# A two-layer block on one core: a batch's Gelu moved into the next batch, the second attention pass unbroken, key rankings back to back

## The reference

```python
# x: (16, 256, 128)
qkv = layernorm(x) @ w_attn                  # 16 query heads of 8 channels, one shared key and value head
att = softmax(causal(q @ k.T / sqrt(8)))     # 256 x 256 for each head
x = x + (att @ v) @ w_proj
xn = rmsnorm(layernorm(x)) * gamma
sim = (xn @ wq.T) against keys               # 8 heads x 2 lists of 32 scores for each token
sx, sy = top16(sim[0]), top16(sim[1])        # the sixteen best of each list
scores, pk = top16(sx + sy over all pairs)   # the sixteen best pairs
h = gelu(xn . table_down[pairs]) * softmax(scores)
x = x + sum over pairs of h * table_up[pairs]
```

## Time and profile before

| | |
|---|---|
| median of three runs | 1045.94 us |
| profiled execution | 1047.43 us |
| its span (first to last instruction) | 1045.6 us |
| DVE busy | 862.4 us (82%) |
| PE busy | 766.0 us (73%) |
| ACT busy | 712.7 us (68%) |
| POOL busy | 644.5 us (62%) |
| chain that ended last, by engine | DVE 38%, PE 34%, issue 16%, ACT 8% |
| mean granted PE clock | 0.887 |

### The profile page before, as it was taken

How to read it: one execution, slowest core, us unless ns; L and a number is a source line. 1 busy time by engine, 2 the same in 40 slices (tenths; PEclk the granted TensorE clock), 3 DMA queues, 4 the chain that set the end, 5 groups by cost and what they waited for, 6 DMA issues and landing times.

```text
span 1045.6 us, 22349 instructions
## 1 busy us (share of the span) xinstructions
PE 766.0 (73%) x6066; PEld 482.5 (46%) x6066; DVE 862.4 (82%) x4054; ACT 712.7 (68%) x1040; POOL 644.5 (62%) x371
## 2 busy tenths in 40 slices
PE   3772868777877878787778878787878778776374
PEld 2431535454554645454455545444545546353243
DVE  2316298998989899899989899989989897988987
ACT  1352686877778686878867786868787786847371
POOL 2111069494958768594939677694949486675851
PEclk9686888899998989898998989898999989897766
DMA  5322103021211103020212112030212111000000
GB/s 148 50 24 35 17 9 43 1 40 15 39 16 35 20 9 47 0 52 3 40 15 39 16 21 34 8 47 0 43 12 39 16 34 18 1 12 2 5 1 10
DMA packets 51538, 26.51 MB, mean 25 GB/s; under 512 B 5168, under 2 KB 51120, under 8 KB 51312
## 3 DMA queue, kind: packets, MB, share of 16 engines
q1 hardware_dynamic: 51504, 26.11, 15.1%
HBM read 19.93 MB, written 5.24 MB: 24 GB/s over the span
## 4 chain that ended last, share of the span: by engine, by line
DVE 38%; PE 34%; issue 16%; ACT 8%; DMA 1%; SPq 1%; POOL 1%; DVEq 1%; ACTq 0%; POOLq 0%
DVE prob L930 13%; PE misc L1156 7%; PE score L1136 5%; PE score L1217 4%; ACT prob L650 4%; DVE late_scores L792 4%; DVE cand_left L894 4%; PE misc L1158 3%; PE score L1138 3%; DVE best L888 3%; DVE best L902 2%; DVE cand L873 2%; PE misc L1245 2%; DVE halves L786 2%; PE score L1229 2%
## 5 line engine op out<-in xcount | busy, mean ns | idle before, releaser
L451 POOL TENSOR_TENSOR acc<-acc,prob 128x1024 f32<-128x1024 f32 x186 | 440.0, 2366 | 16.6 <-DVE prob L930 0.5
L930 DVE SCALAR_TENSOR_TENSOR prob<-score,cut,prob 128x1024 f32<-128x1024 f32 x256 | 317.8, 1277 | 39.3 <-ACT prob L650 38.7
L650 ACT ACTIVATE prob<-score,neg_lse,unit 128x1024 f32<-128x1024 f32 x256 | 296.9, 1198 | 36.2 <-PE score L1217 25.5
L1217 PE MATMUL score<-sel,pieces_t 128*128 128x512 f16 x512 | 176.3, 442 | 73.4 <-DVE prob L930 64.0
L562 ACT ACTIVATE probs<-score 128x512 f32<-128x512 f32 x192 | 107.4, 599 | 65.4 <-PE score L1138 63.8
L438 POOL TENSOR_TENSOR pieces<-sim,pieces 128x512 f16<-128x512 f32 x32 | 36.4, 1159 | 145.1 <-ACT pieces L606 145.1
L1136 PE MATMUL score<-q_stack,k_stack 128*128 128x512 bf16 x192 | 76.3, 401 | 45.7 <-DVE prob L930 23.3
L1217 PEld LDWEIGHTS score<-sel,pieces_t 128*128 128x128 f16 x512 | 42.0, 109 | 145.6 <-DVE prob L930 111.7
L1106 PE MATMUL score<-k_ahead,q_ahead 128*128 128x256 bf16 (+1 forms) x512 | 75.8, 253 | 31.0 <-ACT late_scores L545 13.6
L424 POOL TENSOR_TENSOR scale<-bounded,half_neg 128x2 f32<-128x2 f32 x16 | 11.2, 699 | 130.6 <-DVE bounded L833 130.6
L850 DVE MATCH_REPLACE8 left<-top,sim 128x32 f32<-128x32 f32 x512 | 82.8, 173 | 0.0
(11 more groups left out here) (122 smaller groups left out, 1618.9 us busy)
## 6 DMA issues: line engine op xcount, KB each, us to landing
q_ahead<-q_scratch SPq DMA_DIRECT2D x96, 64.0 KB
q_stack<-q_scratch SPq DMA_DIRECT2D x96, 64.0 KB
q_scratch<-qk_piece SPq DMA_DIRECT2D x16, 192.0 KB, 2.4
xin<-x SPq DMA_DIRECT2D x16, 128.0 KB, 4.4
xres<-x SPq DMA_DIRECT2D x16, 128.0 KB, 4.8
out<-fin SPq DMA_DIRECT2D x16, 128.0 KB, 5.3
k_ahead<-qk_piece SPq DMA_DIRECT2D x96, 4.0 KB
k_stack<-qk_piece SPq DMA_DIRECT2D x96, 4.0 KB
```

What stands on the lines that cost most here:

```text
L451: eng.tensor_tensor(acc[:, j, :], so_far, prob[:, j * FH + h, :], ALU.add).then_inc(acc_added, 1)
L650: eng.activation(prob[:, g, :], score[g % BUFS][:, :], ACT.Exp, bias=neg_lse[:, j, h:h + 1], scale=unit[:, :]).then_inc(prob_made, 1)
L930: eng.scalar_tensor_tensor(prob[:, g, :], score[g % BUFS][:, :], cut[:, j, h:h + 1], prob[:, g, :], ALU.is_ge, ALU.mult).then_inc(prob_mas ...
L1217: ins = eng.matmul(score[g % BUFS][:, cols], pieces_t[:, j, h, :], sel[:, cols], start=True, stop=True)
```

## The change

Six things are done together.

1. The Gelu of batch i is taken in iteration i+1, after the twelve Exps of the second pass, ahead of `invert_sums`. Its matmuls (`hidden_units`) are spread over the second pass: four chunks of tile 1 before the first step, then one chunk after each of the twelve steps, in place of the `keep_busy` matmuls. They read `xn_kept`, a copy of `xn_t`.
2. The two residual copies (`age_x2`, `copy_x2`) and the new copy `keep_xn` are DMAs on SP's queue; they were activations.
3. `weigh_values` waits no longer for `pieces_back`, and no transposes or copies stand inside the second pass. `pieces_back` of both tiles goes in between the first pass's copies, and both use `misc[0]`.
4. On PE `project_y`, the first `piece_transposes` and the first `acc_transposes` stand after two of the first pass's twelve steps; the other ten come behind them.
5. On DVE the rankings of both tiles stand back to back, then `ln1`, `sum_pairs(0)`, `select_pairs(0)`, and only then `make_y`. The gates come later, and `fold_max` comes after `select_pairs(1)` and the second gate, where it stood before `sum_pairs(1)`.
6. In the mask stretch ACT takes `best_exp(1)` before the first `pair_probs`, `log_sum(1)` after it, and spreads the copies of the key scores; on POOL two additions come ahead of `sim_low_piece`.

```diff
@@ SP @@
+            def age_x2(b):
+                copied = held(eng, every(x2_copied, b))
+                read = held(eng, at(fin_made, b, 0))
...
+                eng.dma_start(x2_aged[:, :, :], x2_kept[:, :, :]).then_inc(x2_moved, 16)
+            def keep_xn(b):
+                made = held(eng, every(xn_t_made, b))
+                used = held(eng, at(hidden, b, 0))
...
+                eng.dma_start(xn_kept[:, :], xn_t[:, :]).then_inc(xn_kept_in, 16)
             def iteration(i, d, f, a, m, p):
+                if d and f:
+                    age_x2(i - 1)
+                if f:
+                    copy_x2(i)
@@ ACT @@
                 if a:
-                    for u in range(10):
+                    for u in range(MAX_STEPS):
                         att_exp(i + 1, u)
-                if f:
-                    pieces_back(i, 0)
-                if a:
-                    for u in range(10, MAX_STEPS):
-                        att_exp(i + 1, u)
-                if f:
-                    pieces_back(i, 1)
                 if d and f:
-                    age_x2(i - 1)
-                if f:
-                    copy_x2(i)
+                    activate(i - 1, 0)
+                    activate(i - 1, 1)
                 if a:
                     invert_sums(i + 1)
                 if m:
                     copy_v(i + 2)
-                    for u in range(9):
+                    max_scores_back(i + 2, 0)
+                    max_scores_back(i + 2, 1)
+                if f:
+                    best_exp(i, 0)
+                if m:
+                    for u in range(2, 5):
                         max_scores_back(i + 2, u)
                 if f:
-                    best_exp(i, 0)
+                    pieces_back(i, 0)
+                if m:
+                    for u in range(5, 9):
+                        max_scores_back(i + 2, u)
+                if f:
+                    log_sum(i, 0)
+                    pieces_back(i, 1)
                 if m:
                     for u in range(9, MAX_STEPS):
                         max_scores_back(i + 2, u)
...
+                if f:
+                    best_exp(i, 1)
                     pair_probs(i, 0, 0)
+                    log_sum(i, 1)
                     pair_probs(i, 0, 1)
                 if a:
                     sim_back(i + 1, 0)
+                if f:
+                    pair_probs(i, 0, 2)
+                if a:
                     sim_back(i + 1, 1)
@@ DVE @@
                 if f:
                     select_keys(i, 0)
-                if d:
-                    gate(i - 1, 0)
-                if f:
                     select_keys(i, 1)
                 if p:
                     ln1(i + 3)
-                if a:
-                    make_y(i + 1)
                 if f:
                     sum_pairs(i, 0)
                     select_pairs(i, 0)
                 if a:
+                    make_y(i + 1)
+                if f:
+                    sum_pairs(i, 1)
+                if a:
                     make_x2(i + 1)
                 if d:
+                    gate(i - 1, 0)
+                if f:
+                    sum_best(i, 0)
+                    select_pairs(i, 1)
+                if d:
                     gate(i - 1, 1)
                 if f:
-                    sum_best(i, 0)
+                    log_sum_exp(i, 0)
                 if m:
                     fold_max(i + 2, 0, 6)
                 if f:
-                    sum_pairs(i, 1)
-                    log_sum_exp(i, 0)
-                    select_pairs(i, 1)
-                if f:
+                    sum_best(i, 1)
                     mask(i, 0, 0)
+                    log_sum_exp(i, 1)
                     mask(i, 0, 1)
@@ PE @@
+                if a and d:
+                    hidden_units(i - 1, 1, range(0, 4), xn_kept)
+                for u in range(MAX_STEPS):
+                    if a:
                         scores_for_probs(i + 1, u)
-                        keep_busy(misc[0], 2)
+                    if d and f:
+                        if u < 4 and a:
+                            hidden_units(i - 1, 1, range(4 + u, 5 + u), xn_kept)
+                        elif u >= 4 and a:
+                            hidden_units(i - 1, 0, range(u - 4, u - 3), xn_kept)
...
+                if a:
+                    weigh_values(i + 1, 0, max_t_made, i + 1)
+                    weigh_values(i + 1, 1, max_t_made, i + 1)
+                if m:
+                    scores_for_max(i + 2, 0)
+                    scores_for_max(i + 2, 1)
+                if a:
+                    if f:
+                        eng.wait_ge(pair_step, at(pair_step, i, SUM_STEPS))
+                    project_y(i + 1, y_t_made, i + 1)
+                if f:
+                    if a:
+                        piece_transposes(i, 0, y_t_made, every(y_t_made, i + 1))
...
                 if d:
                     acc_transposes(i - 1, 0)
...
                 if m:
-                    for u in range(4):
+                    for u in range(2, 7):
                         scores_for_max(i + 2, u)
```

More of the change, by code:

```diff
@@ L711, in iteration @@
                     log_sum(i, 0)
+                    pieces_back(i, 1)
+                if m:
+                    for u in range(9, MAX_STEPS):
+                        max_scores_back(i + 2, u)
+                if a:
+                    xn_back(i + 1)
+                if f and not a:
                     activate(i, 0)
                     activate(i, 1)
-                if a:
-                    xn_back(i + 1)
                 if f:
+                    best_exp(i, 1)
                     pair_probs(i, 0, 0)
+                    log_sum(i, 1)
                     pair_probs(i, 0, 1)
@@ L720, in iteration @@
                     sim_back(i + 1, 0)
-                    sim_back(i + 1, 1)
-                if f:
-                    best_exp(i, 1)
                 if f:
@@ L1204, in pair_scores @@
                     eng.wait_ge(piece_t_made, at(piece_t_made, b, j + 1))
-                if g < 2:
+                if g < 2 and not a:
                     eng.wait_ge(act_made, at(act_made, b, g + 1))
+                elif g < 2:
+                    if later(b):
+                        eng.wait_ge(gated, at(gated, b - 1, g + 1))
                 elif g == 2 and m:
@@ new lines, in iteration @@
+                if d and f and not a:
+                    hidden_units(i - 1, 1, range(CH), xn_kept)
+                    hidden_units(i - 1, 0, range(CH), xn_kept)
+                if a:
+                    weigh_values(i + 1, 0, max_t_made, i + 1)
[3 more added lines that the diff above has]
+                    scores_for_max(i + 2, 1)
+                if a:
+                    if f:
+                        eng.wait_ge(pair_step, at(pair_step, i, SUM_STEPS))
+                    project_y(i + 1, y_t_made, i + 1)
@@ L1322, in iteration @@
+                if m:
+                    for u in range(7, 9):
+                        scores_for_max(i + 2, u)
                 if d:
@@ L1324, in iteration @@
                 if m:
-                    for u in range(8, MAX_STEPS):
+                    for u in range(9, MAX_STEPS):
                         scores_for_max(i + 2, u)
+                if f and not a:
+                    hidden_units(i, 0, range(CH), xn_t)
+                    hidden_units(i, 1, range(CH), xn_t)
                 if f:
-                    hidden_units(i, 0)
-                    hidden_units(i, 1)
+                    pair_scores(i, 0, 0, a, m)
+                    pair_scores(i, 0, 1, a, m)
                 if a:
-                    xn_transpose(i + 1, y_t_made, i + 1)
+                    xn_transpose(i + 1, piece_t_made, i)
                 if f:
-                    for h in range(3):
-                        pair_scores(i, 0, h, a, m)
+                    pair_scores(i, 0, 2, a, m)
                 if a:
```

113 lines of the change are left out of this document (46 added, 67 removed).

## The result

| | before | after |
|---|---|---|
| median | 1045.01 us (1043.91 to 1047.60, 4 runs) | 1094.68 us (1092.76 to 1095.91, 4 runs) |
| ratio | | 1.047, 95% interval 1.0444 to 1.0496 |
| span of the profiled execution | 1045.6 us | 1092.8 us |
| DVE, PE, ACT, POOL busy | 862, 766, 713, 645 us | 862, 762, 704, 635 us |
| mean granted PE clock | 0.887 | 0.85 |

The account below looks back on a forecast made before the run. The time to xhat_back plus 20.2 us was taken to set each batch, with late first-pass copies delaying fold_max. Twelve batches 3.4 us longer (40.4) less 2 for edges took 1045.6 to 1084 us; range 1055 to 1098.

Parts of the forecast that it names:

- The ruler: Loop batch: lasts as long as it takes to reach ACT's copy xhat_back, plus an unchanged 20.2 us.
- `make_y` at 17.3: DVE: make_y starts without a wait 17.3 us after the batch's first ranking, against 17.1 before.
- `ln1` 1.17: DVE ahead of make_y: ln1 counted at 1.17 us, its length in the trace of before.
- POOL's additions hold DVE: Rival before make_y: additions ending after 17 hold DVE's two-SBUF steps, 2 us more a batch, 1108 us; chance 0.08.
- The clock: PE's gap before project_y: half rate adds 0 to 1.8 us ahead of the first pass's third step, taken as 1.6.
- everything stays at full clock: Rival on PE: no throttling, fold_max starts at 28.1, a batch is 59.8, total 1065 us; chance 0.22.
- `fold_max` at 29.7: DVE: fold_max starts 29.7 us into the batch, after waiting for ACT's first-pass copies; DVE itself is there at 26.8.
- the sign of 1 us: DVE at fold_max's first step: a new wait of 1 us or more for ACT's copies would show the forecast right.
- The mask stretch: From fold_max's start to xhat_back: 11.55 us, with log_sum(1) and the copies queued behind sum_best(1); xhat_back at 41.2.
- Edges: Iterations 0 and 13 to 15, outside the loop: -3, 0, -3 and +4, together -2 us, bounds -8 and +4.
- The sum: Whole kernel: twelve batches times 3.4 is 40.4, edges -2, so a span of 1084.0 us from 1045.6.
- The costs put at nothing: Residual activations leaving ACT, three DMAs on SP, Gelu matmuls for dummies, Gelu's place: each forecast at no time.

Follow-up runs that it names:

- e1: Kernel after plus 44 dummy matmuls on PE in the gap before project_y; 1068.39 us, ratio 1.0227 to the kernel before.
- e2: Kernel after with best_exp(1) on ACT ahead of the first pass's last three copies and sum_best(1) on DVE ahead of fold_max; 1053.05 us, ratio 1.0085.
- e3: Kernel after with make_y ahead of sum_pairs(0) on DVE again; 1058.52 us, ratio 1.0125.
- e4: Kernel after with the whole of ln1 moved behind make_y on DVE; 1058.89 us, ratio 1.013.
- e5: Kernel after with only ln1's last instruction, the 128x2 tensor_scalar, moved behind make_y; 1080.08 us, ratio 1.0341.
- c13: Kernel after with both the 44 dummy matmuls on PE and make_y ahead of sum_pairs(0); 1057.81 us, ratio 1.0119.
- b_y_late: Kernel before with one edit, make_y moved behind select_pairs(0); 1055.40 us, ratio 1.0088.
- c_best2: c_best, but best_exp(1) behind the first pass's last three copies and sum_best(1) between fold_max's second and third step; 999.48 us, ratio 0.9562.
- c23: Kernel after with best_exp(1) and sum_best(1) early and make_y ahead of sum_pairs(0); 1025.72 us, ratio 0.9811.
- c_best: Kernel after with e2's edit, make_y between sum_pairs(0) and select_pairs(0), and ln1 behind select_pairs(0); 1016.10 us, ratio 0.9724.

## Why the prediction was right, and what was off

The prediction was 1084 with slower at 0.85; measured is 1094.68, inside the range of 1055 to 1098. Step by step:

**The ruler held for this kernel, and not for every one.** From `xhat_back` to the end of the batch it was 20.2 us. It is 20.15 to 20.17 in all twelve batches of before, after, e1 to e5, c13 and b_y_late: after 42.95 and 63.11, e1 40.51 and 60.67, e4 39.50 and 59.66, e5 41.29 and 61.45. So in these the time is set by how soon that copy comes. But 20.16 is the length with PE at half clock behind the copy. In six batches of c_best2 and in some of c23 and c_best it is shorter, down to 18.49, where the clock is full there. In c_best2 that gives about 10 us of its 45 (an estimate: the six differences to 20.16, added up).

**`make_y` at 17.3: wrong by 1.1.** Where: the term "`ln1` 1.17". Its last instruction was in the forecast at the length it has in the trace of before:

```profile
525.29 0.34 DVE L772 TENSOR_SCALAR ln_tmp<-mv 128x2 f32<-128x2 f32 x1
```

That 0.34 was itself a hold, cut short: two of POOL's additions run there from 520.80 for 4.81 us, so one ends at 525.61, where this ends (525.63). Without the gate before it, `ln1` comes 1.1 us earlier in the batch, the additions stay where they were, and the same instruction begins 1.5 us before the addition's end. The rival "POOL's additions hold DVE" had the right mechanism, but its condition was additions that end after 17. They ended at 15.8 as foreseen, and the hold came before that, on an instruction I had not looked at. e5 measures it as 1.1 us a batch. Without it, a batch is 61.46; the prediction's is 61.4. That they agree so closely is in part luck: e5's `make_y` is at 16.9, 0.4 ahead of the forecast, and its `fold_max` 0.1 behind.

**The clock: right, e1.** The forecast added 1.6 for the half rate ahead of the third step. Measured is 1.7: that step begins 3.5 us after `project_y` (678.21 to 681.75), and in e1, at full clock, 1.8 (662.62 to 664.46). The rival "everything stays at full clock" gave 1065, and e1, which makes its condition true, measured 1068. e1's batch of 60.65 less the hold's 1.1 is 59.5 (an estimate, since the hold was measured at half clock), and the rival had 59.8: its arithmetic was right, and its condition false.

**`fold_max` at 29.7: 31.5 in the batch shown.** Of the 1.8, 1.1 is `make_y`, and 0.6 is the third step itself, which also ran at half clock: ACT's first copy comes 1.1 us after it begins (681.75 to 682.85), where 0.5 was forecast. In e5 it is at 29.8. One reading of this step was wrong. The forecast had DVE arrive at 26.8 and wait at `fold_max` for all of the rest, 2.9 us; DVE waits only 0.99 there, just short of the sign of 1 us. It arrives at 30.5, since besides the late `make_y` it stands 0.73 for `project_y` and 0.61 and 1.23 for `acc`'s transposes. These three waits the forecast put at nothing. They don't change its sum, because the copies come last all the same.

**The mask stretch: right in sum, wrong in one releaser.** 11.55 was forecast from `fold_max` to `xhat_back` and 11.49 measured, with ACT's wait of 2.30 for `sum_best(1)`. But the step from the key copy to the fourth `pair_probs`, priced at 1.5 for PE's transposes and `pair_scores` at half clock, took 1.8, and its last 1.25 ended with POOL's first addition. e2 supports that the late masks push this addition back: with the sum early the wait is 0.63 and ends with PE.

**Edges: -7.3 instead of -2.** The -7.3 is inside the bounds of -8 and +4. Up to the loop the gain is 4.7 against 3. From one first ranking to the next, iteration 13 lasts 56.8 for 57.6, iteration 14 52.3 for 57.3, a gain of 5.0 against 3, and from iteration 15 to the end it is 73.5 for 70.4, a loss of 3.1 against 4. The 5.0 fits the wait for y in iteration 14, which was 4.8 before; no run tests it.

**The sum.** Against a predicted span of 1084.0, the loop is 14 us longer (12 times 1.2, of which 1.1 the hold) and the edges are 5 shorter. That gives the 1092.8.

**The costs put at nothing.** The second pass without interruption, the Gelu's place, the three DMAs: `make_y` waits for nothing in the loop, and c_best2, which keeps them all, is the fastest kernel here. So these parts are not what costs; positions are: on DVE `make_y`, `ln1` ahead of it, and `fold_max` ahead of `sum_best(1)`, and on ACT `best_exp(1)`. What brings c_best2's 4.4% was not taken apart, and whether the kernel before would gain as much from a better order of its own was not tried.

By the Trainium skill, "TensorE: Matmul & The Clock Gate", section "Part 1: The HAM clock gate", idleness throttles TensorE, and activity releases it. The trace agrees, by the windows of after and of e1.

## What to carry to other kernels

- A wait is not free time. Before work is put in front of an instruction that waits, follow what stands behind it on the engine that it feeds. Here 5 us of ranking before `make_y` removed 2.6 us of DVE's idleness a batch (the mean of the twelve; 3.7 in the batch of the earlier trace rows) and cost 36 us in all, since ten steps of PE and ten copies of ACT stood behind it.
- Find the one instruction from which the rest of the batch is a fixed length (here `xhat_back` plus 20.16), and judge each edit by whether that comes sooner. Read it in every batch of a variant and not in one: here it holds only while PE's clock behind that instruction stays the same. Then look at what stands in front of a short operation that another engine waits for, as `fold_max` (4.6 us) before a sum of 0.28 us.
- An instruction longer than its size allows, and that ends with another engine's instruction, is being held. Its length in the old trace is a matter of phase, so take its cost anew, up to one whole instruction of the other engine, when it is moved.

## What the runs showed of the hardware

**A tensor_scalar on 128x2 elements is held by a POOL addition.** It takes 0.16 or 0.17 us with POOL free (e4, e5), and 1.48 to 1.55 in the twelve batches of after, beside an addition of 2.4, ending within 0.03 us of it each time. It isn't a late signal of POOL: the one that this instruction needs comes with POOL's norm of the batch before, which ends 57 us earlier (613.9 for 671.23). I had expected a hold only of instructions with two SBUF inputs; this one has one. By the Trainium skill, "SBUF — State Buffer", section "SBUF: two separate sides", a VectorE instruction in a two-port mode contends with GpSimd for the same exclusive pair of ports as one with two SBUF inputs. The trace agrees if that mode is on at so small a size, which is shown here only by the holding.

**Dummy work can pay.** 44 matmuls that nobody reads, 5 us of PE, made the kernel 26 us faster (e1), and nothing where DVE's own work set the start of `fold_max` (c13).

**The same gap does not cost the same each time.** In after most batches last 61.85, 62.7 or 63.1, with a gap on PE of 6.12 to 6.21 in all twelve. The clocks below are those of a short one from 597.42 and of the long one from 659.27. In the short one the granted clock was 0.68 from 13.6 to 17.6 of the batch, where the long one has 1.00, and from 23.6 to 25.6 it was 1.00, where the long one has 0.72. It fell sooner, into the idleness, and came back sooner, for the work.

**The clock behind an unchanged copy made batches of one kernel differ by 1.7 us.** In c_best2 the projection and the next `pair_scores` take the same instructions in each batch, and behind `xhat_back` a batch has 18.49 us left with a granted clock of 1.00 and 20.16 with 0.50.
